# The state recurrence of a decoder kernel spread over all 16 slots of a group

## What is computed

```python
def step(state, inp):
    r_t, k_t, v_t, w_t = inp
    state = state * jnp.exp(w_t)[..., None] + k_t[..., None] * v_t[..., None, :]
    o_t = jnp.einsum('bhkv,bhv->bhk', state, r_t)
    return (state, o_t)
...
dd = sigmoid(tanh(x_shift @ ddlerp_w.T))
lerp = lambda mix: x * (mix + dd * (1 - mix)) + x_shift * (1 - mix - dd * (1 - mix))
r, k, v = proj(lerp(mix_r), r_w), proj(lerp(mix_k), k_w), proj(lerp(mix_v), v_w)
g = silu(proj(lerp(mix_g), g_w));  w = -softplus(-proj(lerp(mix_w), w_w)) - 0.5
out = groupnorm_per_head(scan(r, k, v, w));  return (out * g) @ out_w.T
...
x = x + attn(layernorm(x))                          # the recurrence above
x = x + xattn(layernorm(x), ctx, ctx)               # 16 heads of 64, 128 keys of ctx and 128 learned ones
x = x + moe(layernorm(x))                           # top 2 of 8 experts
```

## Time and profile before

| | us |
|---|---|
| median of three runs | 1756.25 (1752.46 to 1756.86) |
| the profiled execution, own time | 1758.05 |
| its span, first to last instruction | 1756.3 |
| prologue (until the first maximum) | 144.5 |
| groups 0 to 7 of the attention, first maximum to first maximum | 91.4, 100.4, 102.4, 104.6, 105.5, 98.2, 86.2, and 78.8 until the last |
| mean granted TensorE clock | 0.939 of full speed |

### The profile page before, as it was taken

One profiled execution on the slowest core, in us unless ns is written; L12 is line 12 of the kernel. 1 busy time (PEld: TensorE's weight loads), 2 busy tenths in 40 slices (PEclk: granted clock), 3 DMA queues, 4 the chain that ended last, 5 costly groups with the idle time before them and its releaser, 6 DMA issues. The chain is left out here.

```text
span 1756.3 us, 42884 instructions
## 1 busy us (share of the span) xinstructions
PE 1437.4 (82%) x15385; PEld 1068.3 (61%) x15385; DVE 1261.0 (72%) x2773; ACT 1121.4 (64%) x2833; POOL 655.8 (37%) x662
## 2 busy tenths in 40 slices
PE   3158999897988989899882399937889999999995
PEld 1025767676766757677672288834566777776663
DVE  3787979888797978976462555534677988987665
ACT  1026878787877869788780366623667677777663
POOL 1651514434252441511112400042655566554452
PEclk9988999999999999999995599966999999999997
DMA  6352222040412304000000522240000101000000
GB/s 166 89 121 66 61 65 69 20 114 13 106 40 59 88 13 114 15 17 4 18 8 25 184 62 62 60 104 10 21 10 22 35 10 35 24 2 20 21 8 13
DMA packets 77852, 87.56 MB, mean 50 GB/s; under 512 B 11088, under 2 KB 67280, under 8 KB 73296
## 3 DMA queue, kind: packets, MB, share of 16 engines
q1 hardware_dynamic: 70032, 72.58, 16.2%
q0 software_dynamic: 4096, 8.40, 1.7%
q10 hardware_dynamic: 3520, 3.84, 0.7%
HBM read 66.97 MB, written 17.83 MB: 48 GB/s over the span
## 5 line engine op out<-in xcount | busy, mean ns | idle before, releaser
L828 ACT ACTIVATE pr<-P,nm 128x256 f32<-128x256 f32 x512 | 238.3, 492 | 12.6 <-DVE nm L970 12.6
L1860 ACT ACTIVATE et<-P 128x1024 f32<-128x1024 f32 x128 | 131.3, 1026 | 107.5 <-PE P L1676 107.1
L970 DVE TENSOR_REDUCE nm<-P 128x4 f32<-128x1024 f32 x128 | 156.4, 1222 | 52.0 <-PE P L632 36.3
L646 PE MATMUL P<-ident,pr 128*128 128x128 f32 x1024 | 144.2, 286 | 55.9 <-DVE xb L950 32.1
L297 POOL TENSOR_TENSOR rstd<-ve,mhalf 128x4 f32<-128x4 f32 (+2 forms) x80 | 65.2, 816 | 324.9 <-DVE ve L292 324.6
L807 ACT ACTIVATE pr<-pr,ri 128x256 f32<-128x256 f32 x256 | 118.6, 520 | 88.3 <-DVE pr L961 86.9
L816 ACT COPY ptS<-P 128x512 f32<-128x512 f32 x256 | 137.9, 587 | 47.9 <-PE P L646 27.7
L646 PEld LDWEIGHTS P<-ident,pr 128*128 128x128 f32 x1024 | 113.8, 145 | 72.9 <-issue 61.6
L569 POOL TENSOR_TENSOR KV<-KV,kk 128x512 f32<-128x512 f32 x64 | 114.4, 1788 | 49.1 <-DVE nm L970 49.0
L630 PE MATMUL P<-KT,QT 64*128 64x128 f32 x1024 | 127.6, 310 | 4.9 <-ACT pr L828 4.9
L561 POOL TENSOR_TENSOR KV<-KV,R 128x512 f32<-128x512 f32 x64 | 86.9, 1358 | 115.0 <-DVE pr L961 108.4
(11 more groups left out here) (316 smaller groups left out, 4242.6 us busy)
## 6 DMA issues: line engine op xcount, KB each, us to landing
KV<-scr_v SPq DMA_DIRECT2D x16, 1024.0 KB, 7.8
R<-scr_r SPq DMA_DIRECT2D x16, 1024.0 KB, 11.7
xt<-scr_xs SPq DMA_DIRECT2D x71, 64.0 KB, 1.8
scr_ys<-yt SPq DMA_DIRECT2D x71, 64.0 KB, 1.5
x<-in_x SPq DMA_DIRECT2D x8, 256.0 KB
scr_r<-r_out SPq DMA_DIRECT2D x8, 256.0 KB
scr_v<-v_out SPq DMA_DIRECT2D x8, 256.0 KB, 2.0
xb<-in_x SPq DMA_DIRECT2D x8, 256.0 KB, 3.0
```

What stands on the lines that cost most here:

```text
L646: m = nc.tensor.transpose(P[:, 4 + kb, h * T:(h + 1) * T], pr[:, i % 3, h * KEYS + kb * T:h * KEYS + (kb + 1) * T], ident[:, :])
L828: e = nc.scalar.activation(pr[:, s % 3, h * KEYS:(h + 1) * KEYS], scores(s)[:, h // 2, (h % 2) * KEYS:(h % 2 + 1) * KEYS], ACT.Exp, bias=n ...
L970: nc.vector.tensor_reduce(nm[:, s % 3, 0:4].rearrange("p (a h) -> p a h", a=2), scores(s).rearrange("p a (h k) -> p a h k", k=KEYS), AX.X, ...
L1860: nc.scalar.activation(et[:, u % 4, :, :, :], scoresT, ACT.Exp).then_inc(S["h_exp"], 1)
```

## The change

The four steps of chunk j now lie two slots apart for neighbouring j: kv product and scan at offset -31+2j (slots 1, 3, ..., 15), kr product and add at -30+2j (slots 2, 4, ..., 0). POOL thus has one product in each slot, the first of what it does there, and both kinds wait for `b_nd`. On DVE the scan goes from just behind the maximum to the end of the slot. SP stores v ahead of r, and the four loads of a group are issued apart: KV 0-3, R8 0-3, KV 4-7, R8 4-7 at offsets -34, -33, -30, -25, where those of KV 0-3 and R8 0-3 wait for the scan and the kr product that last need these rows. What feeds the recurrence starts earlier: `norm`, `dd`, `v`, `r`, `k`, `w` at -45, -44, -36, -35, -33, -32, so FIRST is -53 instead of -42. `dif` goes from POOL to DVE (slot 6), `dif`*`th` and `now_less` to slot 7, the five mixes to slots 9, 10, 14, 15, 0. The scratch `sq` moves from KV to R8. `setup` stays in slot -27.

```diff
-BANK7 = {"norm": -36, "dd": -35, "r": -32, "v": -30, "k": -29, "w": -28, "g": -24, "o": -15, "og": -10, "out": -9,
+BANK7 = {"norm": -45, "dd": -44, "v": -36, "r": -35, "k": -33, "w": -32, "g": -24, "o": -15, "og": -10, "out": -9,
-FIRST, LAST = -42, UNITS + 25
+FIRST, LAST = -53, UNITS + 25
-            sq, og, on = KV[:, 6, :], R8[:, 6, :], R8[:, 7, :]
+            sq, og, on = R8[:, 5, :], R8[:, 6, :], R8[:, 7, :]
...
+                        sp.wait_ge(S["st_v"], 16 * g + 16)
+                        if g:
+                            sp.wait_ge(S["a_scan"], DH * g - 2)
+                        sp.dma_start(KV[:, 0:4, :], repeated("scr_v", 0)).then_inc(S["rep_v0"], 16)
+                    g = group_at(s, -33)
+                    if g is not None:
+                        sp.wait_ge(S["st_r"], 16 * g + 16)
+                        if g:
+                            sp.wait_ge(S["a_kr"], DH * g - 4)
+                        sp.dma_start(R8[:, 0:4, :], repeated("scr_r", 0)).then_inc(S["rep_r0"], 16)
                     g = group_at(s, -30)
...
+                            sp.wait_ge(S["b7"], filled("o", g - 1))
+                        sp.dma_start(KV[:, 4:8, :], repeated("scr_v", 4)).then_inc(S["rep_v1"], 16)
+                    g = group_at(s, -25)
+                    if g is not None:
+                        if g:
+                            sp.wait_ge(S["b7"], filled("og", g - 1))
+                        sp.dma_start(R8[:, 4:8, :], repeated("scr_r", 4)).then_inc(S["rep_r1"], 16)
...
             def pool_program(pool):
                 for s in range(FIRST, LAST + 16):
+                    for j in range(DH):
+                        g = group_at(s, -30 + 2 * j)
+                        if g is not None:
+                            if 0 < s <= UNITS:
+                                pool.wait_ge(S["b_nd"], s)
+                            pool.wait_ge(S["a_scan"], DH * g + j + 1)
+                            pool.wait_ge(S[f"rep_r{j // 4}"], 16 * g + 16)
+                            nc.gpsimd.tensor_tensor(KV[:, j, :], KV[:, j, :], R8[:, j, :], ALU.mult).then_inc(S["a_kr"], 1)
+                        g = group_at(s, -31 + 2 * j)
+                        if g is not None:
+                            if 0 < s <= UNITS:
+                                pool.wait_ge(S["b_nd"], s)
+                            pool.wait_ge(S["b7_read"], filled("k", g))
+                            pool.wait_ge(S[f"rep_v{j // 4}"], 16 * g + 16)
+                            nc.gpsimd.tensor_tensor(KV[:, j, :], KV[:, j, :], kk[:, :], ALU.mult).then_inc(S["a_kv"], 1)
...
                     g = group_at(s, BANK7["g"])
                         got("g", g)
-                        act.wait_ge(S["a_dif"], 3 * g + 3)
+                        act.wait_ge(S["a_dif"], 3 * g + 5 if g + 1 < GROUPS else 3 * g + 3)
...
-                    g = group_at(s, -42)
+                    g = group_at(s, -53)
                         ln_heads(dve, 0, ALL, x1, "a_mv")
-                    g = group_at(s, -37)
+                    g = group_at(s, -50)
                         ln_tails(dve, 0, ALL, x1, xn, "a_rs", g + 1, "a_xn")
+                    g = group_at(s, -42)
+                        nc.vector.tensor_tensor(b3(dif[:, :]), XS[:, :, 1:T + 1], XS[:, :, 0:T], ALU.subtract)\
+                          .then_inc(S["a_dif"], 1)
-                    for i, (offset, home) in enumerate(((-33, 0), (-32, 1), (-31, 2), (-30, 0), (-29, 1))):
+                    for i, (offset, home) in enumerate(((-39, 0), (-38, 1), (-34, 2), (-33, 0), (-32, 1))):
```

More of the change, by code:

```diff
@@ L482, in sync_program @@
                           .then_inc(S["in_x1"], 16)
-                    g = group_at(s, -31)
+                    g = group_at(s, -35)
+                    if g is not None:
+                        sp.wait_ge(S["b7_read"], filled("v", g))
+                        if g:
+                            sp.wait_ge(S["rep_v1"], 16 * g)
+                        sp.dma_start(d["scr_v"], v_out[:, :]).then_inc(S["st_v"], 16)
+                    g = group_at(s, -34)
                     if g is not None:
@@ L489, in sync_program @@
                     g = group_at(s, -30)
                     if g is not None:
-                        sp.wait_ge(S["b7_read"], filled("v", g))
                         if g:
[L493 to L508, removed]
-                                         bcast(d["scr_r"].rearrange("(h j) n -> h j n", j=DH)[:, part, :]
-                                               .rearrange("h j n -> h (j n)"), 1, DH)).then_inc(S[f"rep_r{half}"], 16)
@@ L552, in pool_program @@
                           .then_inc(S["a_dif"], 1)
[L554 to L569 removed]
+                    g = group_at(s, -53)
+                    if g is not None:
+                        ln_pow(pool, 0, 0, GS, "a_ve", g + 1, "a_rs")
                     g = group_at(s, -9)
@@ L972, in vector_program @@
                                                 AX.X, ALU.max, negate=True).then_inc(S["b_max"], 1)
-                    for j in range(DH):
-                        g = group_at(s, -24 + j)
-                        if g is not None:
-                            dve.wait_ge(S["a_kv"], DH * g + j + 1)
-                            nc.vector.tensor_tensor_scan(KV[:, j, :], dec[:, :], KV[:, j, :], 0.0, ALU.mult, ALU.add)\
-                              .then_inc(S["a_scan"], 1)
-                    g = group_at(s, -42)
+                    g = group_at(s, -53)
                     if g is not None:
@@ L1056, in vector_program @@
                     if g is not None:
[L1057 to L1058 removed]
+                        if g + 2 < GROUPS:
+                            dve.wait_ge(S["b7"], filled("norm", g + 2))
                         else:
@@ L1123, in vector_program @@
                         link(dve, nc.vector.tensor_reduce(gate_b[:, here], gated[:, :, :], AX.X, ALU.add))
+                    for j in range(DH):
+                        g = group_at(s, -31 + 2 * j)
+                        if g is not None:
+                            dve.wait_ge(S["a_kv"], DH * g + j + 1)
+                            nc.vector.tensor_tensor_scan(KV[:, j, :], dec[:, :], KV[:, j, :], 0.0, ALU.mult, ALU.add)\
+                              .then_inc(S["a_scan"], 1)
                     for j in range(1, DH):
-                        g = group_at(s, -23 + j)
+                        g = group_at(s, -30 + 2 * j)
                         if g is not None:
```

50 lines of the change are left out of this document (14 added, 36 removed).

## The result

| | median, us | lowest to highest | runs |
|---|---|---|---|
| kernel before | 1756.43 | 1752.46 to 1756.86 | 4 |
| changed kernel | 1713.62 | 1711.32 to 1716.20 | 4 |

The ratio is 0.9762, 95% interval 0.9742 to 0.9782: 42.8 us faster. The prediction was 1726, within 1706 to 1750; the forecast's own range, 1715 to 1741, is missed by 1.4 us. The profiled span fell from 1756.3 to 1711.6 us.

The account below looks back on a forecast made before the run. No engine was full; different things bound different slots, DVE the long ones, with PE's work as floor. From 1758.05, groups -44.6 and prologue +12 gave 1725.5, taken as 1726; own range 1715 to 1741, 8 in 10 within 1706 to 1750.

Parts of the forecast that it names:

- The middle of a group: Group 3: slot 14 -4.1, slots 12 and 13 -2.9, 10 and 11 -2.3; added scans in slot 5 +1.2, slot 7 +1.1.
- Slots 0 and 15: Group 3: with scatters spread, half of slot 0's excess over 5.85 goes, and a little in slot 15: -1.5 us.
- the step on the new waits: POOL's wait for `b_nd`, ACT's `g` copy and SP's loads in a group: each has time enough; no cost counted.
- Slot 9: Group 3: kv product and bias addition hold DVE until 1.3 us after the maximum; 8.49 to 6.7, -1.8 us.
- the port rule: Whichever of DVE and GpSimd issues first holds the shared port pair for one instruction; slot 9 would cost 1.3 us less.
- The other groups: Groups 2 to 4 together -26.6 us, group 1 -6.4, group 5 -8.2, group 0 -3.4, groups 6 and 7 0.
- The prologue: Before the first maximum: stretches of 44, 53.5 and 57.4 us, first maximum +10.5, taken as +12; bounds -4 to +25.
- the setup's term: Prologue: DVE's setup, 9.2 us, now stands between scans 1 and 2 of group 0: +8 us.
- the deeper one: Rival: slot 0's pause goes altogether and the prologue hides its additions, costing nothing; 1711 us, 17%.
- The port case: Rival: only DVE instructions with two SBUF inputs or fast mode are held; slot 7 +0.3, slot 9 0.4 less; 1720, 18%.
- The shallow one: Rival: PE sets the pace, groups 1 to 5 stop at 100 us each; 1757 us, 7%.
- The slower one: Rival: scatters behind products in slots 1 to 8 of groups 2 to 5 hold DVE's scans or additions; 1768 us, 10%.

Follow-up runs that it names:

- The reordered kernel before: Kernel before, with POOL's `dif` x `th` and `now_less` of slot 14 issued behind that slot's products: 1709.87 us, ratio 0.9867 to the kernel before.
- The read in slot 14: Changed kernel with counts read at the end of slot 14, setup at step -32 and scatters in pairs: 1674.42 us, ratio 0.9663; once more 1672.82, 0.9667.

## Why the prediction was right, and where not

Group 3, slot by slot, predicted and measured on the first chip:

| slots | predicted | measured | |
|---|---|---|---|
| 14 | -4.1 | -4.15 | |
| 12, 13 | -2.9 | -2.88 | |
| 10, 11 | -2.3 | -2.18 | clock part of it |
| 9 | -1.8 | -1.10 | 8th scatter |
| 0, 15 | -1.5 | -2.28, +1.17 | pause gone, bank 7 |
| 5 | +1.2 | +1.28 | |
| 4 | +0.5 | +0.05 | |
| 7 | +1.1 | +0.65 | |
| 1 | +0.5 | +0.56 | |
| 2, 3, 6, 8 | 0 | -1.47 | left out |
| sum | -9.3 | -10.33 | |

**The middle of a group** was right in sign and size: the wait of 3.93 us, the stretched products, the scans in slots 5 and 7. The variant with the kv products behind the maximum shows that the place beside it is worth 24 us, more than half of the gain. The reordered kernel before shows what slot 14's queue alone gives: 21.7 us, against 35.5 for the whole change on that chip. Within groups 0 to 7, without the prologue, it is 19.6 of 47.2.

**Slots 0 and 15** came out near the term by luck, two errors of opposite sign. The pause of slot 0 went altogether on the first chip, where I counted half of it. Slot 15 grew by 1.17 where I had a small gain: in the step on the new waits I went through `b_nd`, `g` and the loads, but not through bank 7, whose k projection now waits for the counts. The order of bank 7's users was in the diff; that step was missing. The read in slot 14 takes the wait away whole.

**Slot 9**: the step named the right pair, the bias addition behind the kv product, but both its size and its premise were wrong. It took both instructions to start with the maximum and the hold to last 1.3 us behind it; a scatter ahead of them put them 1.05 us later, and the mix lost 2.1. I had checked only that nothing waits for the scatter before the next slot, not that POOL's own next product does. And without the scatter the hold is 0.43 and the slot 5.7, not 6.7.

**Of the port rule** (the Trainium skill, "SBUF — State Buffer", section "Who interferes with whom") the part on slot 7 held: there the statistics take 0.87 and 0.36 us beside POOL's products, as they do alone, and the slot costs 0.65, between the 0.3 of that rival and my 1.1. The scan moved into slot 7 was held for one instruction, as that section has it. In slot 9 it doesn't hold: in the changed kernel the mix started 0.21 us after one POOL instruction and was held through that one and the next. When a queue passes the port on and when it doesn't I can't say from these runs: in slot 9 two independent products follow without a gap, in slot 7 `now_less` waits for the instruction ahead of it, but slot 10 of the kernel before has two products in a row and let a scan in.

**The other groups.** Group 0 gained 7.1 instead of 3.4 and holds the largest error. I gave it slot 14's stall less slot 5's growth and little else, but its slots 10 and 11 gained 2.6 (6.13 and 6.40 to 4.99 and 4.96), slot 15 1.5, and slots 0 and 1 1.4, where the clock was 0.50 and 0.73 in slots 0 and 1 and 0.64 in slot 15 before, and the group is at 1.00 now. The clock stands in the windows I used, and no term of the sum has it. On the second chip slots 0 and 1 took 3.96 and 3.97 us in the kernel before too, and group 0 gained 4.6: much of the rest is particular to the trace. Groups 6 and 7 were to stay and gave 2.7, in slots with pauses; on the second chip they gave nothing.

**The prologue** was predicted at +10.5 to +12 and came to +10.6, and its parts held too: the first kv product at 44, then 53.5 to group 1's first, then 57.4 were forecast, and 45.7, 53.3 and 56.1 came. Inside them the terms are off: the setup's term of +8 measured 9.9. The K/V load came 2.3 us sooner for the first product, not 4; the wait for R8 was there (3.30 us idle).

**Sum.** 1725.5 was forecast for the profiled run, and 1713.3 came: of the 12.2 us, 3.7 are group 0, 1.7 group 1, 3.3 groups 2 to 4, 0.6 group 5, 2.7 groups 6 and 7, 1.4 the prologue, less 1.3 in the later phases.

**The rivals.** The time lies nearest to the deeper one (1711), and half of its reason was true: the pause went, but the prologue hid nothing. Its number is met by luck; it gave the prologue 12 us that didn't come, and other slots and groups brought them. The port case (1720) was half true, as said. The shallow one fell: groups 1 to 5 stand at 89.4 to 94.2, not 100, with PE busy for 85.8 to 89.7 of it. The slower one fell: scatters behind the products stretched no scan. It was near in one place, slot 9, with a product and not a scan.

## What to carry to other kernels

Put the work of one engine beside an operation of the other that it doesn't stretch, and pin it there with a wait; here that was worth 24 us for eight of sixteen products. After moving work, list for each shared buffer who is ahead of whom in the new order, and look for one short instruction at the head of a queue: a scatter of 1.06 us cost 1.7 a group, a read of 0.3 us behind a mix cost 1.5. Add to a stall what the slot behind it loses where that slot shows a lower clock.

## What the runs showed of the hardware

- The pause beside scatters goes with the chip in these runs. On the first, PE, DVE and ACT all stop where five to eight scatters follow one another, and the slot is 0.9 to 3.1 us longer (slot 0 of groups 2 to 5 before, slot 0 of group 7 in every kernel); four in a row cost 0.1 over slots 1 to 8 in three groups and 0.5 in one. On the second none stops, with seven. The span of the kernel before is 26.8 us shorter there: 16.6 of it in groups 0 to 7, 10.2 behind them, and only a part of the 16.6 is pauses. What makes the pause is open.
- A pair of scalings of 256 columns, which read them from SBUF, takes 0.62 us alone and 2.08 beside two POOL products; the maximum, which reads PSUM, takes 1.22 beside any.
- The slot behind a stall can lose clock, and not always: behind the same 8.5 us, slot 10 of groups 2, 3 and 4 of one trace (the kernel before on the second chip) runs at 1.00, 0.66 and 0.77 and takes 6.30, 7.93 and 6.74 us.
